# Turning three feature blocks of a second-layer x by DMA moves and starting the feed-forward with two steps together

## What is computed

```
mod = silu(c) @ wmod              # six vectors per batch: sa, ca, ga, sb, cb, gb
h = layernorm(x) * (1 + ca) + sa
x = x + ga * (h @ (weight * mask).T)          # linear layer, 512 x 512, masked by 32 x 32 blocks
h = layernorm(x) * (1 + cb) + sb
x = x + gb * (silu(h @ Wg.T * ag) * (h @ Wu.T * au)) @ Wd.T * ad   # feed-forward, inner size 1376
```

## Time and profile before

| What | Value |
|---|---|
| Median of 3 runs | 177.42 us (176.82 to 177.63) |
| The profiled execution, its own time | 176.95 us |
| Its span (first to last instruction) | 175.2 us, so 1.75 us lie around it |
| PE matmul busy | 168.9 us (96% of the span), 899 instructions |
| DVE, ACT, POOL busy | 100.1, 81.7, 29.8 us |
| Granted PE clock | 0.998 of full speed |
| HBM read | 19.48 MB |

### The profile page before, as it was taken

One profiled execution on the slowest core, in us unless ns is written; L12 is line 12 of the kernel. 1 busy time (PEld: TensorE's weight loads), 2 busy tenths in 40 slices (PEclk: granted clock), 3 DMA queues, 4 the chain that ended last, 5 costly groups with the idle time before them and its releaser, 6 DMA issues.

```text
span 175.2 us, 2553 instructions
## 1 busy us (share of the span) xinstructions
PE 168.9 (96%) x899; PEld 128.8 (74%) x899; DVE 100.1 (57%) x204; ACT 81.7 (47%) x115; POOL 29.8 (17%) x40
## 2 busy tenths in 40 slices
PE   6889999999999999999999999999999999999992
PEld 6855555375568887887788888888888888888881
DVE  6776862894594998324755564427644213442574
ACT  3034002578996957756466443553435524352200
POOL 1333620591049320000000000006500000000000
PEclk9999999999999999999999999999999999999999
DMA  5999997999959402331300000001500000000014
GB/s 175 358 404 402 409 292 241 412 409 404 400 174 314 134 0 50 88 78 31 123 0 6 0 4 0 4 0 60 185 4 0 4 0 4 0 6 0 4 60 180
DMA packets 12389, 23.73 MB, mean 135 GB/s; under 512 B 2920, under 2 KB 5232, under 8 KB 11856
## 3 DMA queue, kind: packets, MB, share of 16 engines
q1 hardware_dynamic: 10864, 22.03, 34.7%
q10 hardware_dynamic: 1504, 1.39, 2.6%
HBM read 19.48 MB, written 2.10 MB: 123 GB/s over the span
## 4 chain that ended last, share of the span: by engine, by line
PE 79%; DMA 7%; SPq 6%; DVE 4%; POOL 1%; issue 1%; ACT 0%; DVEq 0%; POOLq 0%
PE bank L915 46%; PE bank L985 20%; PE bank L883 8%; DMA maskt<-in_att_mask 5%; DMA wffn<-wffn 2%; SPq L241 2%; PE bank L971 2%; PE bank L790 2%; PE bank L862 1%; SPq L263 1%; SPq L256 1%; SPq L250 1%; SPq L253 1%; POOL awork L343 1%; DVE wffn L562 1%
## 5 line engine op out<-in xcount | busy, mean ns | idle before, releaser
L915 PE MATMUL bank<-ht,whi_gu 128*128 128x512 f32 x352 | 83.6, 391 | 0.0
L915 PEld LDWEIGHTS bank<-ht,whi_gu 128*128 128x128 f32 x352 | 65.6, 188 | 13.9 <-issue 0.5
L678 DVE SCALAR_TENSOR_TENSOR awork<-bank,scal,awork 128x512 f32<-128x512 f32 x22 | 16.5, 751 | 50.6 <-PE bank L915 48.2
L985 PE MATMUL bank<-whi_dn,in_split 128*128 128x512 f32 x148 | 37.3, 391 | 0.0
L492 ACT ACTIVATE awork<-bank,scal 128x512 f32<-128x512 f32 x22 | 15.2, 690 | 46.0 <-PE bank L915 46.0
L985 PEld LDWEIGHTS bank<-whi_dn,in_split 128*128 128x128 f32 x148 | 27.6, 188 | 5.9
L883 PE MATMUL bank<-awork,wffn 128*128 128x512 f32 x64 | 31.1, 606 | 0.4 <-ACT wffn L421 0.2
L440 ACT ACTIVATE whi_gu<-wffn 128x1024 fp32r<-128x1024 f32 x22 | 23.3, 1058 | 6.9 <-PE bank L915 6.9
L883 PEld LDWEIGHTS bank<-awork,wffn 128*128 128x128 f32 x64 | 10.7, 190 | 9.9 <-issue 7.4
L687 DVE TENSOR_TENSOR in_split<-awork,in_split 128x512 fp32r<-128x512 f32 x21 | 16.5, 786 | 0.7
L433 ACT ACTIVATE junk<-wffn 128x1536 uint8<-128x1536 uint16 x11 | 16.2, 1477 | 0.9 <-DMA wffn<-in_w_down 0.9
(11 more groups left out here) (72 smaller groups left out, 113.6 us busy)
## 6 DMA issues: line engine op xcount, KB each, us to landing
wffn<-in_w_gu SPq DMA_DIRECT2D x10, 512.0 KB, 8.6
wffn<-in_w_down SPq DMA_DIRECT2D x10, 256.0 KB, 9.4
xt<-in_x SPq DMA_DIRECT2D x8, 256.0 KB, 6.4
modw<-in_mod_ln SPq DMA_DIRECT2D x4, 512.0 KB, 7.3
modw<-in_mod_gate SPq DMA_DIRECT2D x2, 1024.0 KB, 9.6
modw<-in_mod_ln SPq DMA_DIRECT2D x2, 1024.0 KB, 9.2
maskt<-in_att_mask SPq DMA_DIRECT2D x4, 256.0 KB, 8.1
awork<-in_att_w SPq DMA_DIRECT2D x4, 256.0 KB, 8.1
```

The lines of the kernel that those rows point to most:

```text
L678: dve.scalar_tensor_tensor(inner[:, s % 2, :], bank[gu_bank(s, 1)][:, :], scal[:, c, 1:2], silu_g[:, s % 2, :], ALU.mult, ALU.mult).then_i ...
L915: return pe.matmul(bank[gu_bank(s, u)][:, :], w, h, start=(k == 0 and part == 0), stop=(k == KT - 1 and part == 1))
L985: last = pe.matmul(bank[4 + t][:, :], h, w, start=(c == 0 and part == 0), stop=(c == C - 1 and part == 1))
```

## The change

- **Second-layer x of batch 0 (q = 2).** `normalise(2)` writes the first 128 columns of each tile to `xn` as before (counted by `xn_head`) and the other 384 to `xq`, in the place of the first ln2 weights, so it now waits for `rows_done` 4. Nine of the twelve moves are issued by SP ahead of the load of chunk 4 and three by ACT between `copy_rows(3)` and `modulate(8)`; four DVE copies (`keep_second`) do the blocks that stay on their partitions; `transpose_second(1)` to `(3)` on DVE take the place of PE's `transposes(9)` to `(11)`. `transposes(8)` stays on PE.
- **First two steps.** `gate_up_first` does steps 0 and 1 by feature block; `gate_up(1)` goes. ACT rounds both steps' weights ahead of `modulate(9)`.
- **Flags 1 and 2** no longer use PE's sum: SP writes the flag vector to DRAM and reads it back as one row, DVE takes its maximum. Vectors at the start of steps 2 and 5, reads at steps 3 and 6. The first flag's read now stands behind `transpose_second(1)`.
- **Order.** `rows_last`, `columns(3)`, `mask_blocks(2)` and `gate_first(0)` stand one or two linears earlier; mask 2 is loaded ahead of two x tiles; `veps` is made by DVE; `gate_linear(0, 0)` stands ahead of `transpose_first(0)`; ACT's checks are spread differently (the first ahead of `modulate(6)`).

```diff
-CHECKS_AT = {0: 1, 1: 1, 2: 1, 3: 1, 4: 1, 5: 1}
+CHECKS_AT = {0: 1, 1: 2, 2: 1, 3: 1, 4: 1}
+FLAG_VECTOR_AT = {2: 1, 5: 2}
+FLAG_READ_AT = {3: 1, 6: 2}
...
+        def move_second(eng, n):
+
+            i, j = MOVES[n]
+            eng.dma_start(modw[BLK * j:BLK * (j + 1), 1, :, i * P:(i + 1) * P],
+                          modw[BLK * i:BLK * (i + 1), 0, :, j * P:(j + 1) * P]).then_inc(d_second[j], 16)
...
                 if c == TURN_CHUNK:
+                    sp.wait_ge(xn_ok, XN_FIRST + 2 * TT)
+                    for n in range(BY_SYNC_SECOND):
+                        move_second(sp, n)
                     sp.wait_ge(h_ok, 2 * TT)
...
+            def turn_flag(g):
+                sp.wait_ge(flagv_ok, g + 1)
+                sp.dma_start(flag_line[g], flagv[:, g:g + 1]).then_inc(d_flag_out, 16)
+                sp.wait_ge(d_flag_out, 16 * g)
+                sp.dma_start(flagrow[0:1, g, :], flag_line[g:g + 1, :]).then_inc(d_flag_in, 16)
+
+            turn_flag(1)
             sp.wait_ge(xn_ok, XN_FIRST + 3 * TT)
...
+            turn_flag(2)
             sp.wait_ge(grow_ok, 1)
...
             modulate(5)
+            check_chunk(next(check_at))
             modulate(6)
             modulate(7)
             check_chunk(next(check_at))
+            copy_rows(3)
+            act.wait_ge(xn_ok, XN_FIRST + 2 * TT)
+            for n in range(BY_SYNC_SECOND, len(MOVES)):
+                move_second(act, n)
+            modulate(8)
             check_chunk(next(check_at))
-            copy_rows(3)
             check_chunk(next(check_at))
-            modulate(8)
+            round_gu(0)
+            round_gu(1)
             modulate(9)
-            check_chunk(next(check_at))
             modulate(10)
             modulate(11)
-            round_gu(0)
             check_chunk(next(check_at))
             for s in range(STEPS):
-                if s + 1 < STEPS:
+                if 0 < s < STEPS - 1:
                     round_gu(s + 1)
...
+                    if q == 2:
+                        dve.tensor_scalar(xn[:, t, 0:P], src[:, 0:P], mv[:, q, t, 0:1], rstd[:, q, t:t + 1],
+                                          ALU.subtract, ALU.mult).then_inc(xn_head, 1)
+                        dst = xq[:, t, :, 1:KT, :].rearrange("p j k c -> p k j c")
+                        src = src[:, P:D].rearrange("p (k j c) -> p k j c", k=KT - 1, c=BLK)
...
+            def transpose_second(k):
+                if k == 1:
+                    for j in range(GRP):
+                        dve.wait_ge(d_second[j], 16 * (GRP - 1))
+                    dve.wait_ge(kept_second, GRP)
+                    dve.wait_ge(xt_done, 2 * TT + 1)
+                dve.transpose(xturn_second[:, k, :].rearrange("p (t i c) -> p t i c", t=TT, c=BLK),
+                              xb[:, :, :, k, :]).then_inc(xt_done, 1)
...
             normalise(2)
             mod_columns(3)
+            for j in range(GRP):
+                keep_second(j)
             gate_sums(1)
             split(8)
+            flag_vector(0)
+            transpose_second(1)
+            read_flag(0)
+            transpose_second(2)
+            transpose_second(3)
             split(9)
-            flag_vector(0)
-            read_flag(0)
...
-                pe.wait_ge(wgu_hi, 1)
+                pe.wait_ge(wgu_hi, 2)
...
-                    for k in range(KT):
+                    for k, s in ((0, 0), (0, 1), (1, 0), (1, 1), (2, 0), (3, 0), (2, 1), (3, 1)):
...
-                    if (k, t) == (1, 1):
+                    if (k, t) == (1, 0):
                         rows_last()
+                    if (k, t) == (1, 2):
+                        columns(SETS - 1)
                     if (k, t) == (1, 3):
-                        columns(SETS - 1)
-                    if (k, t) == (2, 0):
                         transposes(8)
-                        transposes(9)
-                    if (k, t) == (2, 2):
-                        transposes(10)
-                    if (k, t) == (2, 3):
-                        transposes(11)
-                    if (k, t) == (3, 0):
+                    if (k, t) == (3, 1):
                         pe.wait_ge(modc_ok, SETS)
                         flag_sum(0)
...
-                for g in range(1, len(GROUPS)):
-                    if s == GROUPS[g][0] - 1:
-                        flag_sum(g)
```

More of the change, by code:

```diff
@@ L57 @@
 BY_SYNC = 7
+BY_SYNC_SECOND = 9
 LAG = 2
@@ L121, in adaln_block @@
         flagv = sb("flagv", [P, len(GROUPS)])
+        flagrow = sb("flagrow", [1, len(GROUPS), P])
+        flagmax = sb("flagmax", [1, len(GROUPS)])
         flags = sb("flags", [1, len(GROUPS)], I32)
+        flag_line = nc.dram_tensor("flag_line", (len(GROUPS), P), F32, kind="Internal").ap()
         gates = maskt[:, :, :].bitcast(F32)
@@ L209, in adaln_block @@
         d_turn = [sem(f"d_turn{j}") for j in range(GRP)]
+        d_second = [sem(f"d_second{j}") for j in range(GRP)]
+        kept_second = sem("kept_second")
         checked = sem("checked")
@@ L214, in adaln_block @@
         flag_ok = sem("flag_ok")
+        d_flag_out = sem("d_flag_out")
+        d_flag_in = sem("d_flag_in")
+        flagmax_ok = sem("flagmax_ok")
         wgu_hi = sem("wgu_hi")
@@ L271, in _ @@
             load_att(1)
-            for t in range(TT, NB * TT):
-                load_x(t)
+            load_x(TT)
+            load_x(TT + 1)
             load_mask(2)
+            load_x(TT + 2)
+            load_x(TT + 3)
             load_att(2)
@@ L331, in inverse_deviation @@
                 two = slice(2 * half, 2 * half + 2)
-                pool.wait_ge(stats_ok, TT * q + 2 * half + 2)
-                pool.tensor_scalar(veps[:, q, two], mv[:, q, two, 1], EPS, None, ALU.add)\
-                    .then_inc(veps_ok, 1)
                 pool.wait_ge(veps_ok, 2 * q + half + 1)
@@ L534, in stats @@
                 dve.bn_aggr(mv[:, q, t, :], bns[:, q, t, :]).then_inc(stats_ok, 1)
+                if t % 2:
+                    dve.wait_ge(stats_ok, n + 1)
+                    dve.tensor_scalar(veps[:, q, t - 1:t + 1], mv[:, q, t - 1:t + 1, 1], EPS, None, ALU.add)\
+                       .then_inc(veps_ok, 1)
             def normalise_half(half, tiles):
@@ L578, in transpose_first, with keep_second @@
                    .then_inc(xt_done, 1)
+            def keep_second(j):
+                own = slice(BLK * j, BLK * (j + 1))
+                dve.wait_ge(xn_ok, XN_FIRST + 2 * TT)
+                dve.tensor_copy(modw[own, 1, :, j * P:(j + 1) * P], modw[own, 0, :, j * P:(j + 1) * P])\
+                   .then_inc(kept_second, 1)
+            def transpose_second(k):
[6 more added lines that the diff above has]
+                              xb[:, :, :, k, :]).then_inc(xt_done, 1)
             def transpose_blocks(k):
@@ L665, in read_flag @@
             def read_flag(g):
-                dve.wait_ge(flag_done, g + 1)
-                dve.tensor_scalar(flags[0:1, g:g + 1], bank[3][0:1, 0:1], 0.0, None, ALU.is_gt)\
+                if g == 0:
+                    dve.wait_ge(flag_done, 1)
+                    top = bank[3][0:1, 0:1]
+                else:
+                    dve.wait_ge(d_flag_in, 16 * g)
+                    top = flagmax[0:1, g:g + 1]
+                    dve.tensor_reduce(top, flagrow[0:1, g, :], AX_X, ALU.max).then_inc(flagmax_ok, 1)
+                    dve.wait_ge(flagmax_ok, g)
+                dve.tensor_scalar(flags[0:1, g:g + 1], top, 0.0, None, ALU.is_gt)\
                    .then_inc(flag_ok, 1)
@@ L710, in _ @@
             stats(1, 0)
+            sum_mask(2)
             stats(1, 1)
-            sum_mask(2)
+            keep_blocks(2)
             stats(1, 2)
-            keep_blocks(2)
             stats(1, 3)
@@ L723, in _ @@
             guard_gate(0)
+            gate_linear(0, 0)
             transpose_first(0)
+            for t in range(1, TT):
+                gate_linear(0, t)
             transpose_first(1)
-            for t in range(TT):
-                gate_linear(0, t)
             transpose_first(2)
@@ L744, in _ @@
                         gate_linear(1, t)
-                for g, (first, _) in enumerate(GROUPS):
-                    if s == first - 1:
-                        flag_vector(g)
-                        read_flag(g)
+                if s in FLAG_VECTOR_AT:
+                    flag_vector(FLAG_VECTOR_AT[s])
+                if s in FLAG_READ_AT:
+                    read_flag(FLAG_READ_AT[s])
                 ffn_inner(s)
@@ L853, in transposes @@
                 if k == 0:
-                    pe.wait_ge(xn_ok, XN_FIRST + TT * q if q else TT)
+                    pe.wait_ge(xn_head if q else xn_ok, TT)
                 if n == 2:
                     pe.wait_ge(xn_ok, XN_FIRST)
-                if q == 2 and k < 2:
-                    pe.wait_ge(att_read, k + 1)
+                if n >= 2 * TT:
+                    pe.wait_ge(att_read, 1)
                 elif n >= 2:
@@ L928, in products @@
```

(4 more changed lines are left out.)

31 lines of the change are left out of this document (14 added, 17 removed).

## The result

The changed kernel takes **193.70 us** (median of 6 runs, 192.79 to 195.15) against 177.52 for the kernel before on the same chip: a ratio of 1.091 [95%: 1.085 to 1.097], 16.2 us more. The forecast was 179.0 with a range up to 180.8. The sign was right, and of the size the forecast had a tenth. The profiled execution has a span of 190.8 us (175.2 before) and a mean granted clock of TensorE of 0.973.

What follows compares the result with a forecast made beforehand. TensorE was taken as the bound (79% of the chain of waits). Start +1.1, flag sums -0.9, step 2 +0.3 and flags +1.1 made +1.6 on the median 177.42: 179.0 us, range 176.2 to 180.8.

Steps and rivals of the forecast that it cites:

- the flags' way through DRAM: Ahead of step 4: SP's write and read back take 1.5 us each; PE waits +1.1 (0 to 2.5).
- the second flag: Ahead of step 7: flag there at 35.6, wanted at 35.8 behind the FFN's start, so nothing more.
- the forecast's list of what would be wrong: If the FFN starts before 50.3 or steps 4 and 7 have no gap: moves' issue and landing, or DVE's backlog, failed.
- The start of the FFN: Moves, transpose and flag 0's read set the first FFN matmul: 51.8 instead of 50.7, +1.1 us (50.9 to 52.8).
- ACT's columns: In the linears: ACT waits for check_chunk(0) to 37.1, copy_rows(3) ends at 41.9, PE loses 1.5 us before columns(3).
- The -1.3 of PE's transposes: Ahead of the FFN: twelve transposes no longer on PE, -1.3 us, lying within the later FFN start.
- Flag sums: In the two steps that held flag_sum(1) and flag_sum(2): -0.9 us together, between -0.4 and -0.9.
- Step 2: At step 2's start: PE waits for its weights from ACT, +0.3 us (0.1 to 0.5).
- DVE behind the start: DVE's queue in steps 0 to 2: group 1's flag vector written 14.6 us behind the FFN's start.
- the first rival: Late FFN start but flags in time, by a round trip under 2.5 and no slow DVE operation: 177.9, chance 0.2.
- PE's own end of the linears: Before the FFN: 50.7 - 0.1 - 1.3 + 1.5 = 50.7 (50.3 to 51.0), earlier than the moves' path.

Runs made afterwards that it cites:

- a_pe_flags: The changed kernel with flags 1 and 2 summed by PE and read from PSUM as before; 180.47 us, ratio 1.014.
- c1: The changed kernel, but DVE transposes the flag vector in blocks of 32, so the write to DRAM is 4 pieces of 128 bytes; 181.52 us.
- c2: The changed kernel, but one DMA moves the flag vector within SBUF, in 128 pieces of 4 bytes, without DRAM; 180.37 us.
- b: The kernel before with only the way of flags 1 and 2 changed, through DRAM by SP; 187.32 us, ratio 1.056.
- l: The kernel before with the edits ahead of the second linear, and flags 1 and 2 by one DMA within SBUF without PE's sums; 176.63 us, ratio 0.996.
- f: a_pe_flags with one edit: flag 0 read on DVE ahead of transpose_second(1); 180.84 us, ratio 1.017.
- h: c2 with flags 0 and 1 read earlier, ACT's checks and weight rounding reordered, third transpose behind the first split; 180.19 us, ratio 1.013.
- i: h with SP's nine moves behind two more chunk loads and ACT's check of chunk 4 ahead of modulate(9); 179.71 us, ratio 1.011.
- j: i with eight of the twelve moves issued by SP and four by ACT; 180.12 us, ratio 1.009.

## Why the prediction was right or wrong

**The step that failed is the price of the flags' way through DRAM.** The forecast took 1.5 + 1.5 for it and +1.1 on the path, with bounds up to +2.5. Measured are 7.8 + 3.9, and 13.2 on the path (193.70 - 180.47), on top of the 0.96 for which a_pe_flags waits ahead of step 4 too. The 13.2 hold the clock's share (2.6 in step 4) and are what is left after the flag sums saved. For the second flag the forecast had nothing more; its way took 10.2 instead of 3.4, and step 7 waited 0.95. The row it went by was the nearest in kind (SP, SBUF to DRAM and back), but not in shape: gate_line goes out in 8 pieces of 512 bytes (the kernel writes it by two DMAs, from four partitions each), the flag vector in 128 pieces of 4 bytes. A piece is 128 times smaller, and the upper bound of 3.6, the landing of a large broadcast, didn't reach over it. For a form with no row of its shape the range should have been open upwards, and the forecast's list of what would be wrong named the moves and DVE's backlog, not this way. c1 and c2 show that either change alone would have kept the forecast's order of size: 1.65 + at most 1.9 (c1) and 2.0 (c2).

**A second term was missing:** the wait wasn't paid once. The granted clock fell to 0.50 in it, and step 4 paid 2.6 more (8.15, against 5.57 from 75.48 to 81.05 in a_pe_flags). No rival had it, since none had so long a wait.

**The Trainium skill's pages.** "DMA: Bandwidth & Descriptors" of the Trainium skill, in its section on one DMA's anatomy, gives 2.0 us of fixed cost (fitted there for DMAs that GpSimd issues), and the forecast worked out 4.0 for the round trip by it: nearer than its own 3.0, and still a third of the 11.7 measured. The same page of the Trainium skill has a section "Why small descriptors are slow (HBM only)": transfers within SBUF don't pay the penalty of small pieces. c2 (2.0) against b (6.9) agrees with this. The forecast didn't weigh it; it would have spoken against this change and for c2. What that section names, a fixed cost of some three cycles for each packet and 32 bytes of description for each, gives no price for 128 pieces of 4 bytes. The trace speaks against them as the cause: the packets are through within 0.5 us. Its Specifications say that under 512 bytes an engine reads, modifies and writes; whether that is the cause, no run here shows.

**The start of the FFN** was right: forecast +1.1 at 51.8, measured +1.4 at 52.10 (2.0 by the records). Its parts, changed kernel: second linear at 31.48 (no change forecast, 31.54 before); rows_last at 35.97 (35.9); moves issued from 42.39 (41.7), the last 5.2 later (6.2), landing at 49.66 (49.95); the transpose and the flag:

```profile
49.94 0.71 DVE L634 STREAM_TRANSPOSE modw<-modw 128x512 f32<-128x512 f32 x1 [1.10 <-DMA modw<-modw]
50.58 0.10 DVE L731 TENSOR_SCALAR flags<-bank 1x1 int32<-1x1 f32 x1
```

From the flag's start at 50.58 to the first matmul it was 1.5, of which the forecast's 1.1 (bound 1.5) was to be the whole. Two errors offset each other: the normalisation in eight pieces took 0.84 a tile, not 0.72, and the moves were issued at 0.65 each, not 0.77.

**ACT's columns.** check_chunk(0) waited 2.61 us, to 36.42 (forecast 37.1), copy_rows(3) ended at 41.13 (41.9), and PE lost 0.47 there, not 1.5. Not foreseen was the idle of 1.03 ahead of flag_sum(0), which waits for ACT's fourth check: ACT had stood idle or issued its three moves from 41.13 to modulate(8) at 44.75. Both lie within the start, so the sum didn't change.

**The -1.3 of PE's transposes** lay in the start, as said: with their 1.3 us gone PE had 0.47, 1.03 and 1.01 of idle time instead.

**Slips in the sums.** PE's own end of the linears comes to 50.8 by its terms, not 50.7, and the flag's return to 17.6 (14.6 + 3.0), not 18.0. Neither moved the forecast: the start was set by the moves, the flag by normalise(3) at 18.4.

**Flag sums.** Forecast -0.9 with -0.4 as the other bound; measured 2 x -0.3 = -0.6 (l), since a part of 5.88 - 5.44 is the load that stays.

**Step 2.** Forecast +0.3, measured 0.46 of idle time, 0.7 with the restart of PE.

**DVE behind the start.** The vector was written 15.4 behind the start, forecast 14.6. The slow operation beside POOL came back, 1.67 as in the earlier trace rows, and the cast ahead of it took 1.18, where before it took 0.43 beside POOL's additions too. Changed kernel, then before:

```profile
59.24 1.18 DVE L749 CAST in_split<-awork 128x512 fp32r<-128x512 f32 x1
```

```profile
55.77 0.43 DVE L685 CAST in_split<-awork 128x512 fp32r<-128x512 f32 x1
```

What makes the cast slow in one kernel and not in the other, no run here shows.

In c2, where the flag vector goes out at 67.42 and lands in 2.0, the wait ahead of step 4 is still 1.27: there it isn't the DMA but DVE, which reads the flag behind normalise(3). So a 1.1 ahead of step 4 stays even with a quick way, and the first rival ("flags in time", 177.9) needed more than a short round trip: with quick flags the change gives 180.4.

**Without the flags' term** the forecast would have been 179.0 - 1.1 + 1.3 (c2's wait) = 179.2, against 180.4 in c2: 1.2 low, from step 2's wait (0.84 in c2 for 0.3), the flag sums (0.3) and the start (0.3). So, the clock apart, the mechanisms named were the ones that acted, and the one size that was far off was that of the DMA. That the start came out right is in part luck, by the two errors that offset each other.

## What to carry to other kernels

A DMA is priced by a row with the same piece size and the same kind of destination, not by one with the same byte count: if the trace has none, the upper bound is open, and the cheapest step is to change the shape (one block transpose on DVE) or the destination (SBUF), each of which took the write of the same 512 bytes from 7.8 to 2.0 us or less. Moving a value that gates all of TensorE's work off TensorE saves its 0.3 us and puts a transfer on the path; it pays only where the transfer is short and starts early enough that nobody waits, as in l. And an engine's order repaired at one wait shows the next wait, not the gain: f, h, i and j moved 1 to 2 us between flag, weights and splits. Loads put ahead of small moves lengthen the moves' landing, so what the loads gain the moves can lose.

## What the runs showed of the hardware

- 128 pieces of 4 bytes from SBUF to DRAM: 7.3 to 7.8 us in the changed kernel, 6.9 to 7.2 in b. 4 pieces of 128 bytes to DRAM: 1.6. 128 pieces of 4 bytes within SBUF: 2.0.
- The packets of the 4-byte write to DRAM were all recorded between 68.5 and 69.0, as many and as busy as those within SBUF; from 69.0 to 75.5 the trace has none, and only then was SP released. In b the same: packets until 65.0, release at 70.80.
- SP's moves of 64 KB landed in 2.1 us (median) with the DMA engines 0.09 to 0.29 busy at their start (h), and in 3.5 (i) and 5.1 (j) behind loads that kept them 0.9 to 1.0 busy.
- Reading the 512 bytes back took 3.9 and 2.9 behind the slow writes, and at most 1.9 (DVE was busy until then) and 1.2 behind the packed ones (c1, whose second write took 1.6 like its first); this was measured and not explained.
- In an idle time of 9.93 us PE's granted clock fell from 1.00 to 0.50, and was back at 1.00 some 7 us into the work that followed (0.50 in 84 to 86, 0.83 in 86 to 88, 1.00 in 88 to 90); in one of 6.13 (b) it fell to 0.50 too (16 matmuls in 5.5). In those of 1.27 (c2) and 1.99 (c1) the next 16 matmuls took their usual 3.9.
- From the write of a flag on DVE to the first matmul behind PE's branch: 1.42 (50.68 to 52.10) and 1.28 (79.89 to 81.17), of which the load alone is 0.31 to 0.50.
- Beside POOL's additions the operation of DVE with two tensors in took 1.67 in the kernel before and in the changed one, and 0.69 without them. The cast ahead of it took 1.18 in the changed kernel, 0.76 in c2 and 0.43 before, each beside the same additions: not explained.
